# Transposing the attention weights by a DMA instead of on TensorE, with two output accumulators in PSUM

## The reference

```python
q = einsum('bsd,ed->bse', x, Wq) + bq      # x: (4, 4096, 1024) after layer norm
k = einsum('bsd,ed->bse', x, Wk) + bk      # one head, 1024 wide
v = einsum('bsd,ed->bse', x, Wv) + bv
qk = einsum('bsd,btd->bst', q, k)
theta = 0.5 + 0.2*sigmoid(qk) + 0.15*tanh(qk) + 0.1*relu(qk)
attn = softmax(theta, axis=-1)
out = einsum('bst,btd->bsd', attn, v)
x = x + einsum('bsd,ed->bse', out, Wo) + bo
x = x + relu(layernorm(x) @ W1 + b1) @ W2 + b2   # 1024 -> 4096 -> 1024
```

## Time and profile before

| | us |
|---|---|
| median of 6 runs | 1888.39 |
| lowest and highest | 1882.66, 2120.18 |
| the profiled execution | 1885.4 |
| its span, first to last instruction, slowest core | 1884.3 |
| spans of the 8 cores | 1870.0 to 1884.3 |
| attention stage in it (first scores to last product with the values) | 678.27 to 1182.28 |

### The profile page before, as it was taken

The page is one execution under the profiler, slowest core; times in us unless marked ns, Lnnn a source line. Parts: engine busy times, 40 slices in busy tenths (PEclk is TensorE's granted clock), DMA queues, the critical chain, the costliest instruction groups (busy, mean ns, idle before and its releaser), DMA issues.

```text
span 1884.3 us, 23840 instructions; the slowest of 8 cores (1870.0 to 1884.3 us)
## 1 busy us (share of the span) xinstructions
PE 1472.6 (78%) x9088; PEld 860.7 (46%) x9088; DVE 494.7 (26%) x1008; ACT 764.0 (41%) x1315; POOL 11.7 (1%) x19
## 2 busy tenths in 40 slices
PE   1487775346777779999999999148899888998898
PEld 1376664242333334444444444026365463654654
DVE  0211211103222136565757564011101011010100
ACT  1455554335444445565655554034132140321411
POOL 0000000000000000000000000000000000000000
PEclk8698887677888889999999999569999999999999
DMA  6713899863222100000000000841101011010100
GB/s 75 150 45 106 214 200 193 201 143 94 66 64 64 44 0 7 12 7 12 7 12 7 12 7 12 273 174 34 56 1 56 13 45 57 1 56 12 40 23 23
DMA packets 35857, 123.22 MB, mean 65 GB/s; under 512 B 8610, under 2 KB 8610, under 8 KB 33186
## 3 DMA queue, kind: packets, MB, share of 16 engines
q1 hardware_dynamic: 23650, 71.37, 12.0%
q0 software_dynamic: 9504, 25.17, 8.7%
q10 hardware_dynamic: 2592, 25.17, 3.7%
HBM read 115.41 MB, written 31.46 MB: 78 GB/s over the span
## 4 chain that ended last, share of the span: by engine, by line
PE 68%; DMA 18%; ACT 4%; DVE 3%; issue 3%; ACTq 2%; another core or an unknown queue 1%; DVEq 1%; SPq 0%; POOLq 0%
PE psY L848 12%; PE psH L818 12%; PE psO L611 12%; PE psS L573 11%; PE psV L487 7%; DMA wtmpA<-W 6%; PE psY L755 3%; DMA w_scr<-wtmpA 3%; PE psK L340 3%; ACTq L175 2%; DMA H_sb<-wo_scr 2%; PE psQ L366 1%; DMA xgA<-xb 1%; PE psV L491 1%; DVE PT_sb L559 1%
## 5 line engine op out<-in xcount | busy, mean ns | idle before, releaser
L848 PE MATMUL psY<-W_sb,H_sb 128*128 128x512 bf16 x1024 | 236.5, 391 | 13.5 <-DVE y_sb L860 12.3
L818 PE MATMUL psH<-x2nT,W_sb 128*128 128x256 bf16 x2048 | 225.0, 273 | 0.0
L573 PE MATMUL psS<-K_sb,Q_sb 128*128 128x512 bf16 x1024 | 223.9, 379 | 0.8 <-ACT V_sb L496 0.8
L611 PE MATMUL psO<-V_sb,PT_sb 128*128 128x512 bf16 x1024 | 223.6, 379 | 1.2 <-DVE PT_sb L559 1.2
L818 PEld LDWEIGHTS psH<-x2nT,W_sb 128*128 128x128 bf16 x2048 | 199.7, 98 | 24.8 <-issue 1.8
L829 ACT ACTIVATE H_sb<-psH,b_sb 128x256 bf16<-128x256 f32 x256 | 107.3, 470 | 157.1 <-PE psH L818 157.1
L848 PEld LDWEIGHTS psY<-W_sb,H_sb 128*128 128x128 bf16 x1024 | 100.5, 100 | 140.4 <-issue 32.8
L611 PEld LDWEIGHTS psO<-V_sb,PT_sb 128*128 128x128 bf16 x1024 | 100.1, 98 | 121.9 <-issue 1.3
L573 PEld LDWEIGHTS psS<-K_sb,Q_sb 128*128 128x128 bf16 x1024 | 99.6, 98 | 118.4 <-issue 1.5
L487 PE MATMUL psV<-WvT,xnTB 128*128 128x512 bf16 x512 | 145.5, 435 | 0.0
L860 DVE TENSOR_TENSOR y_sb<-psY,x 128x1024 f32<-128x1024 f32 x16 | 19.6, 1224 | 469.7 <-PE psY L852 469.7
(11 more groups left out here) (91 smaller groups left out, 1360.8 us busy)
## 6 DMA issues: line engine op xcount, KB each, us to landing
xgA<-xb SPq DMA_DIRECT2D x16, 1024.0 KB, 10.2
wtmpA<-W POOLq DMA_DIRECT2D x8, 2048.0 KB, 17.3
w_scr<-wtmpA SPq DMA_DIRECT2D x8, 2048.0 KB, 8.5
xcB<-xb SPq DMA_DIRECT2D x32, 512.0 KB, 4.2
xr_sb<-xb SPq DMA_DIRECT2D x16, 512.0 KB, 4.6
y<-y_sb ACTq DMA_DIRECT2D x16, 512.0 KB, 4.6
On_sb<-on_scr SPq DMA_DIRECT2D x16, 256.0 KB, 3.4
wtmpA<-Wq POOLq DMA_DIRECT2D x1, 2048.0 KB, 20.9
```

The costliest lines, as they stand in the source:

```text
L573: ins = t_eng.matmul(psSs[widx % 4][:], Q_sb[:, ec * QN + i * 128: ec * QN + (i + 1) * 128], K_sb[:, ec * SEQ + w * 512: ec * SEQ + (w + 1 ...
L611: ins = t_eng.matmul(psO[:, half * 512:(half + 1) * 512], PT_sb[:, tci * 128:(tci + 1) * 128], V_sb[:, tci * D + half * 512: tci * D + (ha ...
L818: ins = t_eng.matmul(psHs[icp % 2][:, sub * 256:(sub + 1) * 256], W1_sb[:, hcc * INTER + ic * 128: hcc * INTER + (ic + 1) * 128], x2nT2[vp ...
L848: t_eng.matmul(psY2[:, half * 512:(half + 1) * 512], H_sb[:, ic * 256 + sg * 128: ic * 256 + (sg + 1) * 128], W2_sb[:, ic * D + half * 512 ...
```

## The change

The four TensorE blocks and the four VectorE copies of each tile go. In their place SP issues one DMA with `transpose=True` that reads `P_sb` and writes `PT_sb`, 1024 KB. SP waits before it for the exponential of tile j and for the product of tile j - 1, which read `PT_sb`, and behind it for its landing. The product now waits for the landing, on the new semaphore `ldpt`, and so does the next exponential, since it overwrites `P_sb`. The two PSUM banks that are free become a second output accumulator: `psO2[j % 2]`, so the product of tile j waits for the read-out of tile j - 2. Last, SP now waits for each store of a tile to land before it goes on.

```diff
+    ldpt = E(nc.semaphore("ldpt"))
...
-    psPT0 = s_at.enter_context(nc.psum_tensor("psPT0", [128, 1024], BF16))
-    psPT1 = s_at.enter_context(nc.psum_tensor("psPT1", [128, 1024], BF16))
-    psO = s_at.enter_context(nc.psum_tensor("psO", [128, 1024], F32))
+    psO2 = [s_at.enter_context(nc.psum_tensor(f"psO{i}", [128, 1024], F32)) for i in range(2)]
...
-            for b in range(PB):
-                gidx = j * PB + b
-                if b == 0:
-                    t_eng.wait_ge(sms, exp_ck[j])
-                if gidx >= 2:
-                    pj, pb_ = divmod(gidx - 2, PB)
-                    t_eng.wait_ge(smv, ptev_ck[(pj, pb_)])
...
-                    ins = t_eng.transpose(
...
-                cp = v_eng.tensor_copy(PT_sb[:, b * 1024:(b + 1) * 1024],
-                                       psPTs[gidx % 2][:])
-                v_eng.drain()
-                ptev_ck[(j, b)] = vinc(cp)
+            q_eng.wait_ge(sms, exp_ck[j])
+            if j >= 1:
+                q_eng.wait_ge(smt, av_ck[j - 1])
+            q_eng.dma_start(out=PT_sb.rearrange("p (tc j2) -> p tc j2", tc=TC),
+                            in_=P_sb[:, :], transpose=True).then_inc(ldpt, 16)
+            C["ldpt"] = C.get("ldpt", 0) + 16
+            q_eng.wait_ge(ldpt, C["ldpt"])
...
-            t_eng.wait_ge(smv, ptev_ck[(j, PB - 1)])
-            if j >= 1:
-                t_eng.wait_ge(sms, oev_ck[j - 1])
+            t_eng.wait_ge(ldpt, 16 * (j + 1))
+            if j >= 2:
+                t_eng.wait_ge(sms, oev_ck[j - 2])
...
                 s_eng.wait_ge(smv, recip_ck[i - 1])
+                s_eng.wait_ge(ldpt, 16 * i)
...
             onst_at[j] = C[sok[j % 2]]
+            q_eng.wait_ge(stOns[j % 2], onst_at[j])
```

More of the change, by code:

```diff
@@ L515, in build_nc @@
     psS4 = [s_at.enter_context(nc.psum_tensor(f"psS{i}", [128, 512], F32)) for i in range(4)]
-    psPT0 = s_at.enter_context(nc.psum_tensor("psPT0", [128, 1024], BF16))
-    psPT1 = s_at.enter_context(nc.psum_tensor("psPT1", [128, 1024], BF16))
-    psO = s_at.enter_context(nc.psum_tensor("psO", [128, 1024], F32))
+    psO2 = [s_at.enter_context(nc.psum_tensor(f"psO{i}", [128, 1024], F32)) for i in range(2)]
     t1s, t2s = [t1a, t1b], [t2a, t2b]
     psSs = psS4
-    psPTs = [psPT0, psPT1]
     Ons = [OnA, OnB]
@@ L541, in build_nc @@
         if j >= 0:
-            for b in range(PB):
-                gidx = j * PB + b
-                if b == 0:
-                    t_eng.wait_ge(sms, exp_ck[j])
-                if gidx >= 2:
-                    pj, pb_ = divmod(gidx - 2, PB)
-                    t_eng.wait_ge(smv, ptev_ck[(pj, pb_)])
-                ins = None
-                for kk in range(8):
-                    ins = t_eng.transpose(
[L552 to L558, removed]
-                cp = v_eng.tensor_copy(PT_sb[:, b * 1024:(b + 1) * 1024],
-                                       psPTs[gidx % 2][:])
-                v_eng.drain()
-                ptev_ck[(j, b)] = vinc(cp)
+            q_eng.wait_ge(sms, exp_ck[j])
[5 more added lines that the diff above has]
+            q_eng.wait_ge(ldpt, C["ldpt"])
         if i < TILES:
@@ L611, in build_nc @@
                     ins = t_eng.matmul(
-                        psO[:, half * 512:(half + 1) * 512],
+                        psO2[j % 2][:, half * 512:(half + 1) * 512],
                         PT_sb[:, tci * 128:(tci + 1) * 128],
@@ L644, in build_nc @@
                 s_eng.wait_ge(stOns[j % 2], onst_at[j - 2])
-            ev = s_eng.activation(Ons[j % 2][:], psO[:], AF.Identity,
+            ev = s_eng.activation(Ons[j % 2][:], psO2[j % 2][:], AF.Identity,
                                   bias=0.0, scale=rrow[:])
```

## The result

The changed kernel takes 1846.33 us (median of 5 runs, 1842.79 to 1851.35) against 1888.26 for the kernel before (median of 10 runs): a ratio of 0.9783, 95% interval 0.9752 to 0.9814. In some runs the four cores of one die, or of both, ran at a lower clock; such runs are left out of all ratios (without the two among its ten, the median of the kernel before is 1886.7), and the profile of `plus_half`, which fell in one, is read on a core of the other die.

What follows compares the result with a forecast made beforehand. TensorE was taken to bound the attention stage. Start 8.1, middle tiles 40.9 and end 0.8 - T sum to 49.8 - T, with T = 8 41.8 us less: 1843.6 profiled, median 1847; range 1838 to 2050, the forecast's own 1838 to 1855.

Steps and rivals of the forecast that it cites:

- The bound: Attention stage: TensorE leads; a middle tile takes 30.54 us, 2.92 of it for the transposition, so 40.9 us at most to win.
- The loop through SP: Middle tiles: SP reaches the transposition only behind the store of the tile before, so it is issued 3.46 us after the product.
- The limit of 10.35 us: Middle tiles: longest landing time of the transposing DMA wholly covered by the next scores, 13.81 - 3.46; a tile then takes 27.62.
- T: Time of the transposing DMA from issue to landing, in no profile row; taken as 8 us, between 4.8 and 10.2.
- rival 2: Transposition outlasts the scores, TensorE waits in every tile; at T = 22.5, 143 us more, 2031, up to 2046 with clock; chance 0.25.
- rival 3: Transposing DMA is serial, one engine does the work: 601 us more, or 434 with 32 blocks one after another; chance 0.18.
- the forecast: Transposing DMA lands within 10.35 us, wholly covered in middle tiles: 41.8 us less with T = 8, 1847 us; chance 0.47.
- The second accumulator: Attention stage: removes a product's wait for the read-out of the tile before, which frees nothing by itself; cost and gain 0.
- VectorE's own time for the copies: Middle tiles: four copies of 691 ns leave VectorE; they cost nothing beyond the 2.92 us of the transposition.
- The start and the end: First product of the stage ends 8.1 us sooner; last tile, with no scores to hide behind, gains 0.8 - T, a loss.
- The sum for T above 10.35: Whole stage: gain is 39.5 - 15 x (T - 10.35), over 14 middle tiles and the first product or the last.
- The point of no gain: Landing time of the transposing DMA at which the whole gain is used up: T = 13.0.

Runs made afterwards that it cites:

- plus_half: Changed kernel with half (2048 columns) of each transposition made once more behind its landing; 0.9928 of the kernel before, 29.12 us a tile.
- pe_dummy: Changed kernel with one output accumulator, TensorE again making 32 transposing matmuls per tile that nobody reads; 0.994 of the kernel before.
- dve_dummy: Changed kernel with one output accumulator, VectorE again making its four copies per tile, of leftovers; 0.9799 of the kernel before.
- plus_quarter: Changed kernel with the first quarter (1024 columns) of each transposition made once more behind its landing; 0.9839 of the kernel before, 27.75 us a tile.
- the second comparison: The changed kernel itself, unedited, timed a second time against the kernel before; 0.9801 (0.9772 to 0.983).
- twice: Changed kernel with each transposition made twice, one after the landing of the other; 1.0316 of the kernel before, 34.16 us a tile.

## Why the prediction was right

- The bound. TensorE led the stage, and a middle tile lost exactly the transposition: 2.91 us measured, 2.92 worked out. `pe_dummy` and `dve_dummy` show that it was TensorE's time, with its waits for VectorE's copies in it.
- The loop through SP. 3.46 us from product to issue was read from the end of the old stage; it is 3.5. The limit of 10.35 us held between 9.8 (`plus_quarter`, no wait in 12 of 14 tiles) and 11.1 (`plus_half`, a wait in every tile).
- T. It was taken as 8 and is 6.7. The two rows around it, 4.8 and 10.2, were the right neighbours, but by the formula every T from 4.8 to 10.35 gives a median between 1843 and 1849. Rivals 2 and 3 needed small packets at 10 ns or one engine. The packets are of 256 B and all engines share them. They cost 21 ns each, so the 10 ns read from packets of mostly four bytes was too low a price for them, and the 2.6 us for 4096 of them with it. The 32 blocks take 0.21 us each (6.7 / 32), not rival 3's 1309 ns. The prediction gave these two rivals 0.43 together and the forecast 0.47; the rows of the trace before didn't decide between them, so that T stayed below 10.35 was in part luck too.
- The second accumulator and VectorE's own time for the copies were put at nothing, and are.
- The start and the end were mis-sized by the clock. At the start TensorE stops for 6.84 us and runs at 0.50 for the next 5.9, so the gain is 6.0 and not 8.1. At the end 13.99 was put in for the product, which takes 16.6; with T = 6.7 the loss would have been 5.9 and is 8.8. The prediction had the sign of it, since it priced the slow clock behind a pause of 12.61 us in rival 2, but its own sum, with pauses at the start and the end, left it out. Against the sum, T gave 1.3 us back, and 5.0 were lost at the start and the end. So the stage gained 38.0 us and not 41.8. That the median came out within 1 us of the forecast is partly luck: the medians differ by 41.9, the two profiled spans by 37.4, and the second comparison, 0.9801, gives 37.5.
- Rival 2's price was too low for the same reason: "some 1 us a tile" for the clock is 2.5 on average in `twice` (3.0 in the tile shown, a product of 16.8 us instead of 13.8).
- The sum for T above 10.35 counts a further us 15 times. By the prediction's own terms it is 16: the 14 middle tiles, the last product, and from T = 9.6 on the first one too, which came 2.0 us later in `twice`. The point of no gain would then be T = 12.8 and not 13.0. The real one is lower still: `plus_half`, at 11.1, gained 0.7% and `twice`, at 13.5, lost 3.2%, where the prediction's formula has 8 us. A straight line between these two gives about 11.5, an estimate; nothing was measured between them.

## What to carry to other kernels

Work that moves from the leading engine to a DMA was free here as long as it landed inside work that doesn't need it. Compute this cover from the chain that issues the DMA, with the waits of the issuing queue, and compare it with the landing. Beyond the cover the price is not only the overshoot: pauses of 3.4 to 5.0 us in every tile cost some 2.5 us a tile more in clock here, pauses up to 1.98 us nothing on the core shown, and a pause of 2.27 us nothing or 1.7 us, by core. Look at the first and last round apart, where there is no cover: there the old way may stay the better one.

## What the runs showed of the hardware

- A DMA that transposes 128 x 4096 bf16 from SBUF to SBUF lands in 6.7 us (8.4 at most), a half of it in 4.3 and a quarter in 3.0. It holds the engine that issues it for 4.8 us (1.2 for a quarter) on SP and for 4.9 on ACT, which computes nothing meanwhile; a plain DMA took 0.33.
- Behind pauses of 3.41, 6.84 and 10.49 us TensorE's granted clock was 0.50 for 5.8, 5.9 and 4.6 us. Behind pauses of 1.20 and 1.29 us it stayed at 1.00. In between it depended on the core: behind 1.98 us 1.00, behind 2.00 us 0.71 for 5.8 us, and behind 2.27 us 0.89 on average over the product on six cores and 1.00 on two. Longer ones vary too: behind the 6.84 us of the stage's start it was 0.70 for 5.9 us on core 4 of the changed kernel.
- A store to HBM and a transposing DMA in flight together took 2.3 and 6.8 us instead of 2.0 and 6.7.
